# Graph network block on one Trainium2 core: 16-bit gather rows, row begins in two halves, set-up and message stage joined into one program, index columns copied by ScalarE, message outputs written in feature-major order

## The reference, cut to what matters

```
# layer 0, per edge: xs, xv from x[src] and x[dst]; w from a small MLP of the edge's embedding
s_out, g_out, v_out = products of (xs, xv, directions) with w
edge_ftr = concat([TG*tanh(s_out), TG*tanh(g_out)[:, :, None]*v_out]) * norm[:, None]
x = layernorm(x + segment_sum(edge_ftr, dst))
# layer 1: attention over the same edges
e = leaky_relu(s_src[src] + s_dst[dst]); alpha = softmax of e within each dst
x = layernorm(x + segment_sum(x[src]*alpha[:, None], dst))
```

## Time and profile before

| | us |
|---|---|
| median of 3 runs | 4478.09 (4477.6 to 4480.03) |
| the profiled execution | 4480.86 |
| its span | 4479.1 |
| busy: PE / DVE / ACT / POOL | 3332.8 / 3036.9 / 2154.7 / 3247.6 |
| first stage, to SP's first load of the next | 0 to 377.9 |
| message stage, to its last DVE instruction | 377.9 to 2583.3 |
| the rest | 2583.3 to 4479.1 |

### The profile page before, as it was taken

The page is one execution under the profiler, slowest core; times in us unless marked ns, Lnnn a source line. Parts: engine busy times, 40 slices in busy tenths (PEclk is TensorE's granted clock), DMA queues, the critical chain, the costliest instruction groups (busy, mean ns, idle before and its releaser), DMA issues. The chain is left out here.

```text
span 4479.1 us, 67002 instructions
## 1 busy us (share of the span) xinstructions
PE 3332.8 (74%) x20487; PEld 2103.2 (47%) x20487; DVE 3036.9 (68%) x5225; ACT 2154.7 (48%) x4565; POOL 3247.6 (73%) x3440
## 2 busy tenths in 40 slices
PE   0003888888888888888888802999999999999940
PEld 0001332332332333233323202899999999999940
DVE  4433999999999999999999833344444444444432
ACT  3002555555555555555555310466666666666620
POOL 5776777777777777777777467777777777777766
PEclk9999999999999999999999955999999999999975
DMA  9612222222222222222222112133333333333311
GB/s 334 164 45 45 40 47 49 52 46 47 46 46 47 50 53 47 46 47 46 47 49 52 22 29 56 39 68 77 73 82 74 75 72 73 72 73 72 73 30 26
DMA packets 271192, 283.33 MB, mean 63 GB/s; under 512 B 182593, under 2 KB 236073, under 8 KB 268403
## 3 DMA queue, kind: packets, MB, share of 16 engines
q1 hardware_dynamic: 164150, 207.75, 16.8%
q0 software_dynamic: 106528, 70.98, 10.3%
q10 hardware_dynamic: 462, 4.00, 0.3%
HBM read 192.06 MB, written 90.42 MB: 63 GB/s over the span
## 5 line engine op out<-in xcount | busy, mean ns | idle before, releaser
L628 POOL DMA_INDIRECT edge<-xp_d,idx x1440 | 1420.8, 987 | 537.5 <-issue 393.6
L880 DVE TENSOR_TENSOR prod<-G_ps,hid 128x1000 f32<-128x1000 f32 x1200 | 1399.9, 1194 | 125.6 <-PE G_ps L763 111.3
L1275 POOL DMA_INDIRECT x1e<-tab_d,idxb x1122 | 1100.0, 980 | 342.2 <-issue 337.9
L763 PE MATMUL G_ps<-FT,wst 32*128 32x500 f32 x4800 | 896.6, 633 | 371.0 <-DVE prod L880 367.8
L1324 PE MATMUL G_ps<-tb,hot 128*126 128x442 f32 (+1 forms) x3968 | 799.1, 358 | 0.3 <-DVE x1e L1349 0.2
L1324 PEld LDWEIGHTS G_ps<-tb,hot 128*126 128x126 f32 x3968 | 743.0, 187 | 37.8 <-DVE x1e L1349 1.4
L763 PEld LDWEIGHTS G_ps<-FT,wst 32*128 32x128 f32 x4800 | 246.3, 183 | 807.4 <-DVE prod L880 750.7
L792 PE MATMUL R_ps<-prod,red 128*32 128x500 f32 x4800 | 590.5, 595 | 0.0
L684 ACT ACTIVATE hid<-T_ps 128x500 f32<-128x500 f32 x400 | 233.5, 584 | 721.5 <-PE T_ps L783 688.9
L1324 PE MATMUL T_ps<-tb,hot 128*126 128x442 f32 x2000 | 416.2, 360 | 186.3 <-DVE one_d L1408 186.3
L1324 PEld LDWEIGHTS T_ps<-tb,hot 128*126 128x126 f32 x2000 | 376.6, 188 | 204.9 <-issue 186.4
(11 more groups left out here) (235 smaller groups left out, 4369.5 us busy)
## 6 DMA issues: line engine op xcount, KB each, us to landing
xd_d<-zeros SPq DMA_DIRECT2D x16, 1562.5 KB, 28.6
y_d<-ng SPq DMA_DIRECT2D x40, 595.0 KB
edge<-xp_d,idx POOLq DMA_INDIRECT x1440
xv<-xd_d SPq DMA_DIRECT2D x40, 560.0 KB
y_d<-zr SPq DMA_DIRECT2D x40, 560.0 KB
x1e<-tab_d,idxb POOLq DMA_INDIRECT x1122
edge<-sel_d SPq DMA_DIRECT2D x20, 750.0 KB
edge<-sel_d SPq DMA_DIRECT2D x20, 687.5 KB
```

The costliest lines, as they stand in the source:

```text
L628: nc.gpsimd.indirect_dma_start(out=edge_c[:, i, 8:8 + DIM], out_offset=None, in_=xp_d, in_offset=bass.IndirectOffsetOnAxis(col, 0)).then_i ...
L763: return Tn.matmul(G_ps[pair][:, a * 512:a * 512 + GW], wst[rows, r * 128:(r + 1) * 128], FT[k][rows, :], start=True, stop=True)
L880: V.tensor_tensor(prod[b][i][:, :].rearrange("p (a e) -> p a e", a=2), gv, hid[k][:, :].rearrange("p (a e) -> p a e", a=1).broadcast_to([1 ...
L1275: nc.gpsimd.indirect_dma_start(out=gx[b][:, c * T1:(c + 1) * T1], out_offset=None, in_=tab_d, in_offset=bass.IndirectOffsetOnAxis(idx[b][: ...
```

## The change

What it does:

- **16-bit rows.** The destinations are cast to int16 as well (`dst16`), stored as `dst16_d`, and the 100 fine gathers fetch 800 bytes per partition into `blk16` instead of 1600.
- **Row begins in halves.** `first_i` of nodes 1 to 99 is made from `endf` shifted in SBUF, nodes 1 to 49 in the middle of the fine counts, 50 to 99 after them. Only node 0 still needs `startf` from DRAM. The scatters are issued as 1 to 49, 50 to 99, 0.
- **Order on POOL.** `endh` and the fifth `early` piece move from before the scatters to behind them.
- **One program.** First and message stage are one block. SP issues the message stage's loads other than `xv` when its part of the first stage has ended (`a_out` at 97, after `sel_d` has landed), then waits for the scatters, then loads `xv`. ACT and DVE wait for `a_out` at 97. `xp` is moved (`room`) so that no tile of the message stage lies on it.
- **Index columns.** ACT copies the 8 columns in `high`, ahead of its three copies of the piece; POOL's copy and its wait go.
- **`post` in feature-major order.** L900 and L906 run through features outside and columns inside; they write runs of 8 adjacent words and read `pb` with a step of 24 words, `pg` with 8, `th` with 16 from element to element.

```diff
-        dstf_d = dram("dstf_d", (NSB, SB))
+        dst16_d = dram("dst16_d", (NSB, SB), mybir.dt.int16)
-        src_i = sb("src_i", [PG, EP], i32)
+        src_i = sb("src_i", [PG, EP + 2 * PW], i32)
+            dst16 = sbt("dst16", [P, EP], mybir.dt.int16)
+            blk16 = sbt("blk16", [PG, NF * SB], mybir.dt.int16)
+            room = sbt("room", [128, 300])
...
             def first_gpsimd(pool):
...
-                    early(EARLY - 1)
-                    pool.wait_ge(S("a_start"), 32)
-                    nc.gpsimd.indirect_dma_start(out=endh[:, :], ...
-                    pool.wait_ge(S("a_idx"), 1)
-                    pool.wait_ge(S("a_xd0"), 16 * NZ)
-                    for k in range(NP):
+                pool.wait_ge(S("a_xd0"), 16 * NZ)
+                for half_no, ks in enumerate((range(1, NPH), range(NPH, NP), range(1))):
+                    pool.wait_ge(S("a_idx"), half_no + 1)
+                    for k in ks:
                         nc.gpsimd.indirect_dma_start(out=xd_d, out_offset=bass.IndirectOffsetOnAxis(first_i[:, k:k + 1], 0), ...
-                    pool.wait_ge(S("a_xd"), 16 * NP)
-                    pool.wait_ge(S("a_hx"), 16)
-                    pool.wait_ge(S("a_endh"), 16)
-                    pool.wait_ge(S("a_link"), 1)
+                pool.wait_ge(S("a_start"), 32)
+                nc.gpsimd.indirect_dma_start(out=endh[:, :], ...
+                early(EARLY - 1)
...
+                def starts(k0, k1, start):
+                    step(V.tensor_tensor(empty[:, k0:k1], endf[:, k0:k1], start, ALU.is_equal))
+                    V.scalar_tensor_tensor(first_i[0:P, k0:k1], empty[:, k0:k1], float(E), start, ALU.mult, ALU.add).then_inc(S("a_idx"), 1)
...
+                V.tensor_copy(dst16[:, :], dst_i[:, :]).then_inc(S("a_dstf"), 1)
...
+                    if k == NPH + NF - 1:
+                        step(V.scalar_tensor_tensor(endf[:, 0:NPH], tn[:, 0:NPH], float(SB), fine[:, 0:NPH], ALU.mult, ALU.add))
+                        starts(1, NPH, endf[:, 0:NPH - 1])
...
 # message stage, SP
                     for h in range(2):
-                        load(h, h)
+                        load_rest(h, h)
                         load_post(h, h, 0)
+                    sp.wait_ge(S("a_xd"), 16 * NP)
+                    for h in range(2):
+                        load_rows(h, h)
 # POOL
-                                if c == 0 and not fixed:
-                                    nc.gpsimd.tensor_copy(idx[:, i:i + PW], src_i[:, bass.ds((p + RING) * PW, PW)]).then_inc(S("b_ix"), 1)
-                                    hold(S("b_ix"), p - RING + 1)
 # ACT
+                    act.wait_ge(S("a_out"), 97)
...
+                        if fetch:
+                            A.activation(idx[:, s * PW:(s + 1) * PW], src_i[:, bass.ds((p + RING) * PW, PW)], ACT.Copy)
 # DVE
+                    dve.wait_ge(S("a_out"), 97)
+                    dve.wait_ge(S("a_hx"), 16)
...
-                            V.scalar_tensor_tensor(ov[:, :, 0:8], thv[:, :, 0:8], TG, nrm, ALU.mult, ALU.mult).then_inc(S("b_gs"), 1)
+                            V.scalar_tensor_tensor(of[:, 0:8, :], thv[:, :, 0:8].rearrange("p c w -> p w c"), TG,
+                                                   nmp[h][:, c0:c0 + PW].rearrange("p (w c) -> p w c", w=1).broadcast_to([P, MO, PW]),
+                                                   ALU.mult, ALU.mult).then_inc(S("b_gs"), 1)
-                            V.tensor_tensor(ov[:, :, 8:32].rearrange("p c (w a) -> p c w a", a=3), pbv,
-                                            pgv.rearrange("p c (w a) -> p c w a", a=1).broadcast_to([P, PW, MO, 3]), ALU.mult).then_inc(S("b_o"), 1)
+                            V.tensor_tensor(of[:, 8:32, :].rearrange("p (w a) c -> p w a c", a=3), pbv.rearrange("p c w a -> p w a c"),
+                                            pgv.rearrange("p c (w a) -> p w a c", a=1).broadcast_to([P, MO, 3, PW]), ALU.mult).then_inc(S("b_o"), 1)
```

More of the change, by code:

```diff
@@ L207, in gnn_resnorm_kernel @@
             iot_s = sbt("iot_s", [128, 1])
+            room = sbt("room", [128, 300])
+            xp = sbt("xp", [PG, NP * DIM])
             ssel, psel, ksel = [sq[:, a * NSEL:(a + 1) * NSEL] for a in range(3)]
             selT = [blkbuf[0:SELB, a * 4 * P:(a + 1) * 4 * P] for a in range(2)]
[L211 to L296, removed]
-                    for k in range(NP):
-                        if k % NPH == 0:
-                            pool.wait_ge(S("a_blk"), k // NPH + 1)
-                        if k >= NF:
-                            pool.wait_ge(S("a_fine"), k - NF + 1)
-                        nc.gpsimd.indirect_dma_start(out=blkbuf[:, (k % NF) * SB:(k % NF + 1) * SB], out_offset=None, in_=dstf_d,
-                                                     in_offset=bass.IndirectOffsetOnAxis(blk_i[:, k:k + 1], 0)).then_inc(S(f"a_fg{k % NF}"), 16)
-                    early(EARLY - 1)
-                    pool.wait_ge(S("a_start"), 32)
-                    nc.gpsimd.indirect_dma_start(out=endh[:, :], out_offset=None, in_=end_d,
-                                                 in_offset=bass.IndirectOffsetOnAxis(idx1[:, :], 0)).then_inc(S("a_endh"), 16)
-                    pool.wait_ge(S("a_idx"), 1)
-                    pool.wait_ge(S("a_xd0"), 16 * NZ)
-                    for k in range(NP):
@@ new lines, in first_tensor @@
+            def first_tensor(pe):
+                pe.wait_ge(S("a_id"), 2)
+                pe.wait_ge(S("a_ones"), 1)
+                pe.wait_ge(S("a_diag"), 1)
+                for a in range(2):
+                    last = nc.tensor.matmul(G_ps[0][0:P, a * 512:a * 512 + NSB // 2], ones[0:P, 0:P], blkbuf[0:P, a * NSB // 2:(a + 1) * NSB // 2], start=True, stop=True)
+                last.then_inc(S("a_hrow"), 1)
+                pe.wait_ge(S("a_diag"), 2)
+                nc.tensor.matmul(R_ps[0:P, 0:P], ones[0:P, 0:P], diag[:, :], start=True, stop=True).then_inc(S("a_hrow"), 1)
+                pe.wait_ge(S("a_w2x"), 9)
+                for o in range(NR * MO):
+                    last = nc.tensor.transpose(G_ps[0][:, o * HID:(o + 1) * HID], w2x[:, o * 128:(o + 1) * 128], ident[0:HID, 0:HID])
+                last.then_inc(S("a_wt"), 1)
+                pe.wait_ge(S("a_link"), 1)
+                nc.tensor.transpose(Y_ps[0:P, 0:P], link[:, :], ident[0:P, 0:P]).then_inc(S("a_linkT"), 1)
+                pe.wait_ge(S("a_sel"), 2)
+                for a in range(2):
+                    for b in range(4):
+                        last = nc.tensor.transpose(T_ps[a][0:SELB, b * P:(b + 1) * P], (psel, ksel)[a][:, b * SELB:(b + 1) * SELB], ident[0:P, 0:P])
+                    last.then_inc(S("a_selp"), 1)
@@ L558, in _ @@
                 def _(sp):
+                    first_sync(sp)
                     def hold(s, n):
@@ L568, in load, with load_rows, load_rest @@
                             hold(S("b_fs"), ch * NPC - NPC)
+                        load_rows(ch, h)
+                        load_rest(ch, h)
+                    def load_rows(ch, h):
                         by_rows(sp, xv[h][:, :], xd_d.rearrange("(p c) f -> p (c f)", c=EP)[:, bass.ds(ch * C * DIM, C * DIM)], S(f"b_ld{h}"))
+                    def load_rest(ch, h):
                         by_rows(sp, em[h][:, :], emb.rearrange("(p c) f -> p (c f)", c=EP)[:, bass.ds(ch * C * NEMB, C * NEMB)], S(f"b_ld{h}"))
@@ L608, in _ @@
                 def _(pool):
+                    first_gpsimd(pool)
                     def hold(s, n):
@@ L702, in turn @@
                                 s = (g + 4) // 2
-                                high(t * RING + s, s % RING, t * 2 + s // PC)
+                                high(t * RING + s, s % RING, t * 2 + s // PC, not last and not (first and s < RING))
                             if not (last and h == 1):
@@ L748, in _ @@
                 def _(pe):
+                    first_tensor(pe)
                     Tn = nc.tensor
```

388 lines of the change are left out of this document (226 added, 162 removed).

## The result

| | before | after |
|---|---|---|
| median, on the same chip | 4477.85 (4474.99 to 4480.03, 4 runs) | 4507.73 (4505.35 to 4509.71, 4 runs) |
| ratio, 95% interval | | 1.0066 (1.0051 to 1.0081) |
| span of the profiled execution | 4479.1 | 4506.2 |
| DVE's first multiply of the message stage | 403.15 | 394.77 |
| DVE's last instruction of that stage | 2583.13 | 2605.17 |

The stage starts 8.4 us sooner and is 30.4 us longer. The last 5 us of the 27.1 lie where no code was changed; this rest took between 1894.7 and 1900.9 us in the twelve profiles of the experiments, whatever the kernel, so they belong to the execution and not to the change. Two things went the other way: the waits of the earlier trace rows, 3.7 us, are gone, and the last two waits for ACT's `th` took 3.8 us together where they took 7.0. That makes 29 of the 30.4.

The account below looks back on a forecast made before the run. DVE and TensorE trade the pace in the message stage; POOL is the chain in the first. -2.5 (start), -2.7 (index copy) and +18 (`post`) sum to +12.8 on 4478.1, giving 4491 us, range 4452 to 4522.

Parts of the forecast that it names:

- slower as the likeliest of three: Whole kernel: slower by more than 0.2% (9 us) had chance 0.48, against faster 0.32 and within that 0.20.
- one hop paid: L906: only one of its two stepped reads costs, 0.44 us to the next start; 4480 to 4503 us, chance 0.42.
- both reads pay: L906: both stepped reads cost, 2.5 ns an element or more; 4513, up to 4527 us, chance 0.15.
- the order of `post`: L906, message stage: stepped reads hold DVE 0.44 us instead of 0.35, 0.09 more times 200, +18 us.
- The row of L1375: Profile row of a read at 33 words, 237 against 201 ns for 40 elements; used to price L906's reads.
- both operands pay one after the other: Upper end for L906: both reads' costs add to 0.27 + 0.35 = 0.62 us to the next start, +54 us.
- That a hop in a read holds DVE more than one in a write: L906: its write hop holds DVE up only 0.08 us; a late read holds the stream and counts whole.
- L900 inside the even half's wait: L900, 64 elements: at most 0.06 us more, hidden in DVE's 0.28 us wait for TensorE.
- Start of the message stage: First stage into message stage: loads hang on `endh`, so ACT starts at 383.0 against 385.51; -2.5 us, from +5 to -17.
- the stall of the fine gathers: POOL, first stage: 800-byte rows shrink the 21.8 us lost to late landings by 7.5 us, ends 0 and -21.8.
- Waits for POOL near the end: End of message stage: ACT's index copy removes DVE's waits of at most 3.7 us; -2.7 us taken.
- a joined program that gains in full: Start of message stage: loads don't hang on `endh`, ACT starts at 356.5, -29 us; 4464 us, chance 0.05.

Follow-up runs that it names:

- experiment 8: Changed kernel with DVE's selection work done before its wait for `endh` and `fix_i` made last; 4485.1 us, ratio 1.0017 to the kernel before.
- experiments 9: Kernel before with only the 16-bit rows (one more cast, fine gathers of 800 bytes); 4472.3 us, ratio 0.9986 to the kernel before.
- 2: Kernel before with only the new order of `post`, both instructions; 4515.2 us, ratio 1.0079 to the kernel before.
- 10: Changed kernel with the index columns copied by POOL again; 4510.3 us, ratio 1.0061 to the kernel before.

## Why the prediction was right, and where its terms were off

It said 4491, in a range of 4452 to 4522, and slower as the likeliest of three. Measured was 4507.7. The direction was right, and for the right reason: the reads of the new L906 cost more than its writes saved, and the start of the message stage hangs on `endh`. But the time lies above the 4480 to 4503 that the prediction gave to its likeliest case, one hop paid, and nearer to the 4513 of "both reads pay", which it gave 0.15. And all three terms of the sum were off, two in size and one in its cause. Two of the errors partly cancel: the order of `post` cost twice its price, 18 us more, and the start gained 6 us more. That the total lies only 17 us off is in part luck.

- **The order of `post`: +18 forecast, +36 measured.** The term that was mis-sized is the price of L906's new reads, "I take the one hop, as the nearest row has it". The row of L1375 is a hop of 33 words and gave 0.9 ns an element. The price depends on the step, and not by its length alone: by the durations it is 0.8 ns an element at 8 words, 1.4 at 24 and 1.1 at 25. A hop of 8 words costs 0.15 us here over runs, close to the forecast's 192 x 0.0009 = 0.17, but `pb` is read at 24 words, and that costs 0.26: the next start comes 0.53 us later and not 0.44. The upper row, "both operands pay one after the other", was near in size (0.62) and wrong as a mechanism, since the second hop is free beside the first.
- The Trainium skill, on the page "Vector Engine (DVE) Microarchitecture Reference", in the section on measured stream behaviour on trn2, gives 2.50 ns an element for both sources stepping 24 words; the prediction worked 0.55 us out of it, and 0.53 was measured. The rows above add that one source at 24 words is enough for it.
- **That a hop in a read holds DVE more than one in a write** is shown: L906's hop of 41 words in what it writes held DVE 0.08 us, that of L924 with 8 words 0.07, and a read at a step 0.15 to 0.26, all over runs. Of the writes' extra duration (0.17 and 0.15 us) about half holds up the next instruction, of the reads' all.
- **L900 inside the even half's wait**: right; 0.04 us more, taken out of the 0.28.
- **Start of the message stage: -2.5 forecast, -8.4 measured.** The mechanism was right: the loads hang on `endh`, and experiment 8 gives back some 22 us by taking them off it. The size was not, and the prediction had named it as a sign of being wrong if ACT's start moved by far more than 3 us. The parts were off nearly all one way: the stall of the fine gathers gave 8.8 us, not 7.5 (136.8 us for 99 steps where it was 145.6); the cast cost 0.7, not 1.0 (71.46 against 70.78); the scatters took 136.8 us from the start of the first to the end of the last where it was 138.0, since one was held a microsecond less; `endh` landed 1.25 us after the end of its issue, not 3; from L432 to the first load it took 11.8 us, not 13.2; and the twelve loads before `xv` took 10.5 us, not 11.8. Only `xv` went the other way, 5.7 us from its issue to ACT's start and not 4.3: its landing was priced by `kp`'s, which is a load of 140 KB where `xv` has 560.
- **Waits for POOL near the end: -2.7 forecast as the index copy's gain.** This step was wrong. The waits are gone, but they are as well in the kernel before with 16-bit rows and in the kernel before with the new order of `post`, where POOL still copies, and the copy put back at POOL costs nothing (experiments 9, 2 and 10). Why the one profile of the kernel before has them stays open.
- The rival of a joined program that gains in full was put at 0.05 and -29 us at ACT's start; the order of the waits took it away. Experiment 8 shows that it was there to be had: with the loads off `endh`, ACT starts at 356.63, 28.9 us before the kernel before.

## What to carry to other kernels

An elementwise operation that has to transpose somewhere should hop where it writes and run where it reads, and hop in the instruction that stands in front of a wait. Look at the time from its start to the next start, not at its duration. Before a stage is joined to the next one, follow what each engine's first wait of the new stage hangs on: one small transfer at the end of POOL's queue held back twelve loads that didn't need it, and the one behind them. Prices of access patterns from a neighbouring row hold only for the same step.

## What the runs showed of the hardware

**The step of a read matters, and steps don't add.** 192 elements at 8, 25 and 24 words cost 0.15, 0.20 and 0.26 us over runs of 8 adjacent words; a second operand at 8 words beside the last two adds less than 0.01. Padding a column from 24 to 25 words takes 0.30 to 0.32 us from a chunk, some 12 us over the 40 chunks; by the ratios it gave 8 and 15. Two operands at 24 words were not run.

**A DVE `tensor_tensor` with both inputs in SBUF holds up POOL's indirect DMA.** DVE's timeline of the kernel after, beside which the scatters at 219.94 and 242.14 take 5.16 and 5.09 us:

```profile
219.10 5.14 DVE L417 TENSOR_TENSOR sq<-dirv 125x4800 f32<-125x4800 f32 x1
...
241.22 5.16 DVE L421 TENSOR_TENSOR dirv<-dirv,rn 125x4800 f32<-125x4800 f32 x1
```

The scatter that is being issued ends 0.86 and 0.85 us after DVE's operation. Length alone doesn't do it: beside the reduce of 5.15 us and the reciprocal of 10.15 us that stand between the two, and have one operand each, the scatters take 0.98. Whether it is the number of inputs or the kind of operation was not separated. In the kernel before with 16-bit rows it was `endh`, a gather, that took 6.38 us there. The Trainium skill, on the page "SBUF — State Buffer", in the section "Who interferes with whom", says that a DVE instruction with two SBUF inputs contends with a GpSimd instruction that reads SBUF, and tells of a probe in which `tensor_tensor` did not stall a DMA, for a reason that it infers. Here it did: 5.16 and 5.09 us for a scatter of 0.98. Cutting both operations in eight gave 6.9 us back on POOL; beside the pieces of 0.8 us a scatter takes up to 1.54.
